# 48 products of a tile of ones on TensorE ahead of the first context's products

## The reference

```
g_x     = g_w @ x_2 + g_b            (then transposed)
theta_x = theta_w @ x + theta_b      (then transposed)
phi_x   = phi_w @ x_2 + phi_b
W       = theta_x @ phi_x / 1024
y       = (W @ g_x) transposed
wy      = w_w @ y + w_b
wy      = bn_gamma * (wy - bn_mean) * rsqrt(bn_var + 1e-5) + bn_beta
out     = wy + x
```

## Time and profile before

| | |
|---|---|
| median of 3 runs | 796.55 us (795.48 to 796.59) |
| the profiled execution, its own time | 797.28 us |
| its span, first to last instruction | 795.5 us |
| TensorE (PE) busy | 778.5 us, 98% of the span |
| GpSimd (POOL) busy | 540.8 us, 68% |
| VectorE (DVE) busy | 524.7 us, 66% |
| ScalarE (ACT) busy | 305.4 us, 38% |
| mean granted clock of TensorE | 0.998 of full speed |

### The profile page before, as it was taken

How to read it: one execution, slowest core, us unless ns; L and a number is a source line. 1 busy time by engine, 2 the same in 40 slices (tenths; PEclk the granted TensorE clock), 3 DMA queues, 4 the chain that set the end, 5 groups by cost and what they waited for, 6 DMA issues and landing times.

```text
span 795.5 us, 11592 instructions
## 1 busy us (share of the span) xinstructions
PE 778.5 (98%) x4045; PEld 665.4 (84%) x4045; DVE 524.7 (66%) x889; ACT 305.4 (38%) x514; POOL 540.8 (68%) x358
## 2 busy tenths in 40 slices
PE   4999999999999999999999999999999999999997
PEld 4688888888888888888888888888888888888886
DVE  3787584857758497584857758497584857758254
ACT  3734442325334143442325334143442325334131
POOL 4969785777857579585777857579585777857500
PEclk9999999999999999999999999999999999999999
DMA  9828255171643707255171633707255171630202
GB/s 235 195 107 211 107 117 201 33 219 67 167 150 73 243 0 211 105 115 201 31 220 65 167 149 73 243 0 211 105 117 200 29 223 64 168 150 1 106 1 105
DMA packets 55127, 103.17 MB, mean 130 GB/s; under 512 B 2474, under 2 KB 37956, under 8 KB 55108
## 3 DMA queue, kind: packets, MB, share of 16 engines
q1 hardware_dynamic: 52976, 101.86, 43.7%
q10 hardware_dynamic: 2132, 1.05, 0.8%
HBM read 69.35 MB, written 33.55 MB: 129 GB/s over the span
## 4 chain that ended last, share of the span: by engine, by line
PE 96%; DVE 2%; ACT 1%; DMA 1%; issue 0%; DVEq 0%; SPq 0%; ACTq 0%
PE wbank L667 56%; PE gbank L667 36%; PE wbank L830 1%; DMA ctx_sb<-in_ctx_dram 1%; PE wbank L708 1%; PE wbank L686 0%; ACT ctxT_hi L340 0%; DVE x_sb L486 0%; PE wbank L714 0%; ACT x_sb L366 0%; DVE ctxT L486 0%; DVE th_lo L583 0%; DVE tmp L509 0%; DVE tmp L508 0%; ACT x_hi L340 0%
## 5 line engine op out<-in xcount | busy, mean ns | idle before, releaser
L286 POOL TENSOR_TENSOR ctxT_lo<-ctxT,ctxT_hi 128x512 fp32r<-128x512 f32 x124 | 167.6, 1353 | 200.1 <-ACT ctxT_hi L340 200.1
L297 POOL TENSOR_TENSOR ctx_sum<-ctx_sum,ctxT 128x512 f32<-128x512 f32 x108 | 163.7, 1516 | 0.2
L315 POOL TENSOR_TENSOR x_lo<-x_sb,x_hi 128x1024 fp32r<-128x1024 f32 x60 | 142.4, 2406 | 0.0
L340 ACT ACTIVATE mt<-wbank 128x512 fp32r<-128x512 f32 x64 | 37.9, 597 | 242.7 <-PE wbank L667 242.7
L657 DVE SCALAR_TENSOR_TENSOR x_sb<-wbank,const,x_sb 128x512 f32<-128x512 f32 x112 | 79.2, 747 | 67.6 <-PE wbank L667 67.6
L667 PE MATMUL wbank<-ctxT_lo,ctxT_hi 128*128 128x512 f32 x512 | 121.0, 392 | 0.0
L518 DVE TENSOR_TENSOR stage<-gbank,mt 128x384 f32<-128x384 f32 x64 | 28.3, 485 | 139.8 <-PE gbank L667 139.7
L667 PEld LDWEIGHTS wbank<-ctxT_lo,ctxT_hi 128*128 128x128 f32 x512 | 95.1, 189 | 18.6 <-POOL ctxT_lo L286 0.2
L340 ACT ACTIVATE ctxT_hi<-ctxT 128x512 fp32r<-128x512 f32 x124 | 76.5, 628 | 87.9 <-DVE ctxT L486 87.9
L667 PE MATMUL gbank<-ctxT_hi 128*128 128x384 f32 (+1 forms) x512 | 80.5, 313 | 10.2 <-ACT ctxT_hi L340 10.2
L667 PEld LDWEIGHTS gbank<-ctxT_hi 128*128 128x128 f32 x512 | 79.8, 191 | 12.0 <-issue 10.2
(11 more groups left out here) (107 smaller groups left out, 1363.3 us busy)
## 6 DMA issues: line engine op xcount, KB each, us to landing
x_sb<-in_x_dram SPq DMA_DIRECT2D x16, 2048.0 KB, 7.8
out_dram<-x_sb SPq DMA_DIRECT2D x64, 512.0 KB, 2.6
ctx_sb<-in_ctx_dram SPq DMA_DIRECT2D x60, 512.0 KB, 8.5
ctx_sb<-in_ctx_dram ACTq DMA_DIRECT2D x4, 256.0 KB, 7.4
ctx_sb<-in_ctx_dram SPq DMA_DIRECT2D x4, 256.0 KB, 7.3
x_sb<-in_L_xattn_w_w_dram SPq DMA_DIRECT2D x1, 512.0 KB, 11.8
stage<-in_L_xattn_theta_w_dram SPq DMA_DIRECT2D x1, 512.0 KB, 12.7
phi_nat<-in_L_xattn_phi_w_dram SPq DMA_DIRECT2D x1, 512.0 KB, 12.8
```

What stands on the lines that cost most here:

```text
L286: nc.gpsimd.tensor_tensor(ctxT_lo[:, c, :], turned_ctx(b, c), f(ctxT_hi[:, c, :]), ALU.subtract).then_inc(sem_, 1)
L297: nc.gpsimd.tensor_tensor(ctx_sum[:, :], ctx_sum[:, :], src, ALU.add).then_inc(ctxT_used, 1)
L315: nc.gpsimd.tensor_tensor(x_lo[:, k, :], x_sb[par][:, k, :], f(x_hi[:, k, :]), ALU.subtract).then_inc(x_lo_made, 1)
L340: nc.scalar.activation(dst, src, ACT.Copy).then_inc(sem_, 1)
```

## The change

Behind the wait for `ones_done`, TensorE multiplies the tile of ones by itself 48 times, 128 columns each, into the first 128 columns of `wbank[0]`. Each product starts the bank anew; nobody reads the result. These stand ahead of everything else on TensorE. Line numbers behind the change grow by two and then by five.

```
--- before.py
+++ after.py
@@ -58,6 +58,8 @@
     Q_BANK = [1, 2]
     T_ORDER = [2, 3, 1, 0]
 
+
+    WARM_UP = 48
     NW = 5
     NO = KC * NH
     NT = KI * NH
@@ -715,6 +717,9 @@
                                            stop=k == KI - 1)
                 ins.then_inc(zb_done, 1)
 
+            pe.wait_ge(ones_done, 1)
+            for i in range(WARM_UP):
+                mm(wbank[0][:, 0:P], ones_r[:, :], ones_r[:, :], True, True)
             pe.wait_ge(ident_r_made, 1)
 
             def body(b, half, par, nxt, nxt2):
```

## The result

The changed kernel takes 797.27 us (median of 22 runs, 796.57 to 797.59), the kernel before, on the same chip, 795.61 (22 runs, 795.13 to 796.94): a ratio of 1.0018, 95% interval [1.0012, 1.0024]. The change makes the kernel 1.7 us slower by the medians and 1.4 by the ratio (which goes by means): less than the 2% at which these comparisons speak of slower, but clear of the measurement.

What follows compares the result with a forecast made beforehand. TensorE holds 96% of the last chain, but its early chunks matter only up to 14.5 us. Products, wait and bank 0, block -0.16: 796.55 - 0.16 = 796.4 us; range 795.2 to 797.7.

Steps and rivals of the forecast that it cites:

- the pace of the 48 products: TensorE's start: 17 products slow at 0.217 us, 31 fast at 0.116, end at 8.9; cost 0.
- Two of the signs that were to show the prediction wrong: From the list of wrong signs: first context product after 10.9 (warm-up too long); PE at full clock through 27 to 31.
- The evidence against the rival: TensorE, 28 to 31 us: only 128-column transposes with the same gaps for loads, yet full clock behind them.
- The rival that came true: TensorE's start: ones don't raise the clock, products end at 12.1, first chunk 1.9 us late; 798.4 us, chance 0.07.
- The path: First 32 us: TensorE's chunk work matters only up to the transpose of the vectors, ending 14.52; after that it has slack.
- The cap: VectorE before chunk 4: context's second half lands at 15.0, so of 1.29 us lead only 0.16 remain.
- the lead going through: Chunk 4: second half lands by 13.9, block moves up to 1.3 us; 795.2 us, chance 0.12; sign: turned before 14.5.
- The clock's fall before 27 us: TensorE before the weight transposes: idle grows 1.9 to about 3.0 us, clock falls more often; +1.1, 797.5 us, chance 0.14.
- race: VectorE's L503 against GpSimd: losing 0.02 us ends it 1.2 later, `scale` about 1.6 late; 798.1 us, chance 0.07.
- The level of before: Whole kernel: 796.55 us, from runs at 795.48, 796.55 and 796.59; the forecast subtracted 0.16 from it.
- The class, no change: Whole kernel: time neither below 794.96 nor above 798.14 us, chance 0.79.

Runs made afterwards that it cites:

- varied128_n36: Changed kernel with 36 fp32r products of 128 columns of a tile of varied numbers in place of the 48 of ones; 796.06 us, ratio 1.0006.
- ones256_n36: Changed kernel with 36 products of 256 columns of ones in place of the 48 of 128; one run, 795.09 us.
- turn128_n36: Changed kernel with 36 transposes of the float32 identity, 128 columns, in place of the 48 products; 796.39 us, ratio 1.0013.
- f32prod128_n16: Changed kernel with 16 float32 products of 128 columns of ones in place of the 48 in fp32r; one run, 796.25 us.
- before_vec_early: Kernel before, no products of ones, with the transpose of the vectors behind chunk 0's gbank products instead of chunk 1's; 795.03 us, ratio 0.9988.
- ones512_n17: Changed kernel with 17 products of 512 columns of ones in place of the 48 of 128; 796.48 us, ratio 1.0009.
- ones512_keep: ones512_n17 with nine more of its products at the head of `turn_w`, into `wbank[3]`, filling TensorE's idle time; 795.30 us, ratio 0.9995.
- n48_vec_early: Changed kernel, all 48 products, with the transpose of the vectors behind chunk 0's gbank products instead of chunk 1's; 795.74 us, ratio 1.0000.
- idle_start: Kernel before, no products of ones, with TensorE waiting for the second ctxT_lo before its first product; 797.85 us, ratio 1.0025.

## Why the prediction was wrong

**The step that failed** is the pace of the 48 products: "I take the lag that PE showed from its first product to full speed, 3.6 us: 3.6/0.217 = 17 products slow, 31 x 0.116 = 3.6 us fast, end at 8.9." All 48 were slow. The end at 12.2 is the upper bound that the same paragraph worked out (12.1) and the chances gave 0.07. Two of the signs that were to show the prediction wrong came: the first context product after 10.9, and TensorE at full clock through 27 to 31. The lag had been read from products of 384 and 512 columns and carried over to a shape that, at the start, no row of before shows. varied128_n36 and ones256_n36 show that the width decides it in fp32r, turn128_n36 and f32prod128_n16 that the width alone does not. Nor is the lag one number where the clock does rise: with the context products of before it was over 6 us in before_vec_early (9.89 to past 16.1), and the same 17 products of 512 columns took 5.84 us in ones512_n17 and 6.45 in ones512_keep.

**The evidence against the rival misled.** I held that the transposes between 28 and 31 us had brought the clock back with "the same gaps for loads". True of these transposes: turn128_n36 shows them raising it. But fp32r products of the same width and spacing do not. Two instructions with the same rows in the timeline were not the same for the clock. Of transposes the Trainium skill ("TensorE: Matmul & The Clock Gate", Part 4) says that full clock does not engage for them. The measurement differs from it and decides: 36 of them went from half to full clock here, in 5.48 us where 36 products of ones took 7.94.

**The rival that came true** was priced at 1.9 us and the loss is 1.7 by the medians, 1.4 by the ratio. It took everything behind the first context product to be late by as much as that product, 1.78 us. In the profiled executions the transpose of the vectors was late by 1.32 only: the first two groups, at half clock in both, took 2.88 us instead of 3.15, and the third, in which the clock rises, 0.73 instead of 0.92. L499 gave back 0.22 more, since GpSimd was already idle when it came (0.17 against 0.39), so chunk 4 was turned 1.10 late. The medians lie further apart because neither profiled execution is a typical one. The changed kernel's took 796.94, 0.33 under its median; that of before, less the 1.5 for the fall, would be at 795.8, 0.2 over its own. That is an estimate, and 1.10 + 0.33 + 0.2 makes 1.6.

**The path was right.** Lateness reaches the end through L675 alone: moved by one chunk it costs next to nothing (n48_vec_early), and without any products of ones lateness costs as it does with them (idle_start: the transpose of the vectors 0.42 later than in the changed kernel, the loss 0.5 to 0.6 larger). TensorE's slack behind the transpose of the vectors is real: its chunks end later in n48_vec_early than in the changed kernel (26.2 against 26.0), for no loss.

**The cap was right.** With a warm-up that works, or the transpose moved early, VectorE waits 1.19 and 1.95 us for the second half of the context. The landing is not fixed at 15.0, though: where chunk 4 waits for it, it is turned at 14.15 to 14.84. In ones512_n17 that is 14.31, ahead of the 14.5 that was to be the sign of the lead going through, but the first half had landed early too (7.86 against 8.68), and VectorE did wait. So that rival falls in these profiles; the time of a working warm-up, level with before, fits this.

**The clock's fall before 27 us was right as a mechanism and stood with the wrong kernel.** It became more frequent with a TensorE that is early: nine of eleven runs of ones512_n17, at 1.1 to 1.2 us, priced at 1.1. The changed kernel is late and idles 1.70 us, and in none of its 22 runs is the mean granted clock below 0.999. No race was lost: L505 takes 0.12 in it, and its counterpart in every other profile of this case too.

**The level of before** was off too: 796.55 is the median of three runs, two of which sit 1 us above the 795.6 that 22 gave. So the predicted 796.4 was a forecast of a time 0.8 above the real level of before, though it was meant as 0.16 below that level. That the 797.27 lies inside the range is luck: the range reached up to 797.7 for a fall of the clock that did not come, from a level that was 0.9 too high. The class, no change, is not what the interval says.

## What to carry to other kernels

A warm-up has to be checked by its own spacing: if the last dummy product stands as far from its neighbour as the first, it warmed nothing, and every one beyond the first real operand is a delay. Look for the one instruction on the warmed engine that another engine waits for; moving that transpose by one chunk gave 0.12% by the ratio, half of it for want of falls of the clock, where warming the engine gave nothing. And an engine that gets ahead idles somewhere else, where the clock can fall: ask for the next gap before filling the first.

## What the runs showed of the hardware

- From half clock, 36, 48 and 60 products of 128 columns in fp32r did not raise TensorE's clock, whatever the data (ones, varied). 36 of 256 columns at the same spacing did (16 matmuls in 3 us for both), so did 17 of 512, 36 float32 transposes of 128 and 16 float32 products of 128. The Trainium skill ("TensorE: Matmul & The Clock Gate", the table on why this matters) advises a warm-up with matmuls for a benchmark, in a row that names no shape; here the width and the format decided.
- An operation of four elements on VectorE took 0.17 beside an idle GpSimd (L499 in the kernel after) and 1.11 behind an operation of GpSimd that had just begun (L499 in n48_vec_early). The Trainium skill ("SBUF — State Buffer", the reading of the diagram) calls the shared ports a lock held for a whole instruction, and both rows agree.
- The column of the granted clock shows 1.00 in 2 to 7 us of the kernel after, where 25 matmuls of 128 columns stand, and in 10 to 13.35 of before, where the spacing says half in both. In this case's profiles it has to be read by the spacing ahead of its first change.
- TensorE's clock fell ahead of the weight transposes in some executions of a kernel and not in others: in 16 of 73 runs of before (idle 1.91 us in the profiled one) and nine of eleven of ones512_n17 (idle 0.32 and 2.30), by a mean granted clock below 0.999; in none of 22 of the kernel after (idle 1.70) and none of eleven of before_vec_early (idle 0.16).
